# Inverse roots of five norms: one power on GpSimd instead of a root on ScalarE and a reciprocal on VectorE

## The reference

```
h = maximum(layernorm(x), 0)                       # norm 1: (x - m) / sqrt(v + eps)
x = x + L0(h, edges, edge_weight)                  # three gin layers: segment sums and small matmuls
h = maximum(layernorm(x), 0)                       # norm 2
x = x + L1(h, edges, node_vec)
L1: for three layers:                              # widths 256, 256, 128
      res = x @ aw + ab
      x = gat(x, src, dst, gw, a_s, a_d, gb) + res # attention over each node's edges, 8 heads
      x = silu(g * (x - mean) * rsqrt(var + eps) + b)   # batch norm
    x = x @ out_w + out_b
```

## Time and profile before

| | |
|---|---|
| median of 3 runs | 5514.25 us (5514.02 to 5518.28) |
| the profiled execution | 5531.82 us, span 5530.3 us |
| busy: TensorE, VectorE | 2609.5 us (47%), 2382.5 us (43%) |
| busy: ScalarE, GpSimd | 595.1 us (11%), 2781.9 us (50%) |
| table loads on ScalarE at the root's line L688 | 5, of 1283 ns each |

### The profile page before, as it was taken

How to read it: one execution, slowest core, us unless ns; L and a number is a source line. 1 busy time by engine, 2 the same in 40 slices (tenths; PEclk the granted TensorE clock), 3 DMA queues, 4 the chain that set the end, 5 groups by cost and what they waited for, 6 DMA issues and landing times. The chain is left out here.

```text
span 5530.3 us, 62828 instructions
## 1 busy us (share of the span) xinstructions
PE 2609.5 (47%) x13804; PEld 1907.7 (34%) x13804; DVE 2382.5 (43%) x7342; ACT 595.1 (11%) x1968; POOL 2781.9 (50%) x2942
## 2 busy tenths in 40 slices
PE   1666774354545445446355444445543333333333
PEld 1555542123333333334233333333432332332323
DVE  5888513324444444442444444444423333333333
ACT  2222300110000000003000000000020000000001
POOL 2000011356666666663566666666446666666663
PEclk9777887667677766778767677777765555555555
DMA  2222563033333333332333333333312221222222
GB/s 61 106 103 90 242 218 156 26 81 88 89 89 89 89 90 88 91 88 46 81 91 88 89 89 88 88 88 90 67 34 45 47 47 45 47 46 46 46 47 21
DMA packets 246618, 451.19 MB, mean 82 GB/s; under 512 B 163452, under 2 KB 165314, under 8 KB 241709
## 3 DMA queue, kind: packets, MB, share of 16 engines
q0 software_dynamic: 122928, 318.15, 23.6%
q1 hardware_dynamic: 111150, 128.71, 6.9%
q10 hardware_dynamic: 12384, 2.25, 0.3%
HBM read 392.07 MB, written 57.21 MB: 81 GB/s over the span
## 5 line engine op out<-in xcount | busy, mean ns | idle before, releaser
L495 POOL DMA_INDIRECT rows_all<-gat_tab,ell x2664 | 2517.2, 945 | 1566.2 <-issue 799.4
L1003 PE MATMUL banks<-rows_all,ident 128*128 128x264 f32 (+1 forms) x5328 | 1795.9, 506 | 2272.9 <-PEq L119 1791.5
L1003 PEld LDWEIGHTS banks<-rows_all,ident 128*128 128x128 f32 x5328 | 1305.8, 286 | 2763.1 <-issue 2576.9
L1575 DVE COPY lrel<-m_all 128x8 f32 x666 | 133.9, 201 | 1536.2 <-issue 1201.8
L1600 DVE TENSOR_TENSOR rows_all<-rows_all,banks 128x1024 f32<-128x1024 f32 (+1 forms) x666 | 685.7, 1042 | 218.8 <-issue 142.7
L789 ACT ACTIVATE banks<-ex_in 128x40 f32<-128x40 f32 x666 | 138.3, 208 | 3771.3 <-ACTq L119 2499.9
L1553 DVE TENSOR_TENSOR acc<-acc,banks 128x264 f32 (+1 forms) x675 | 259.7, 385 | 469.3 <-DVEq L119 278.1
L1546 DVE TENSOR_TENSOR acc<-acc,banks 128x264 f32 (+1 forms) x675 | 258.0, 382 | 107.0 <-issue 102.3
L859 PE MATMUL banks<-rows_all 128*128 128x52 bf16 x4992 | 187.5, 202 | 157.0 <-PEq L119 151.6
L495 POOL DMA_INDIRECT edges<-sw_d,edge_pick x28 | 34.6, 1236 | 412.5 <-POOLq L119 400.5
L859 PEld LDWEIGHTS banks<-rows_all 128*128 128x128 bf16 x4992 | 176.9, 108 | 182.3 <-issue 181.6
(11 more groups left out here) (276 smaller groups left out, 1974.2 us busy)
## 6 DMA issues: line engine op xcount, KB each, us to landing
rows_all<-gat_tab,ell POOLq DMA_INDIRECT x2664
x_t<-adj_d SPq DMA_DIRECT2D x11, 3328.0 KB
y_t<-adj_d SPq DMA_DIRECT2D x11, 3328.0 KB
adj_d<-x_t SPq DMA_DIRECT2D x7, 3328.0 KB, 10.0
adj_d<-y_t SPq DMA_DIRECT2D x6, 3328.0 KB, 9.8
ell<-ell_d SPq DMA_DIRECT2D x666, 2.5 KB
acc<-key_d SPq DMA_DIRECT2D x1, 1664.0 KB, 6.4
acc<-vec_d SPq DMA_DIRECT2D x1, 1664.0 KB, 18.6
```

Source lines behind the costliest of these rows:

```text
L495: return g.indirect_dma_start(out=dst, out_offset=None, in_=table, in_offset=bass.IndirectOffsetOnAxis(ap=idx, axis=0))
L1003: last = t.matmul(sum_ps[u % SUMS][:, 0:width], ident[:, :], rows[u][:, r * width:(r + 1) * width], start=(r == 0), stop=(r == SLOTS - 1))
```

## The change

GpSimd gets a function `inverse_root`, called five times: behind the 26 gathers of norm 1, behind the 26 gathers of norm 2, and at the end of each attention layer. It waits for the signal (now `root_in`), raises the variance elementwise to a tile of -0.5 and signals `root_done`. VectorE's reciprocals go; the Newton step stays, on the power's result. ScalarE's `sqrt` goes in all five places. In the batch norms a SiLU of one column into an unused tile `warm` stands in its place, so that SiLU's table is loaded there.

```
+        minus_half, warm = sb("minus_half", [P, T]), sb("warm", [P, 1])
...
@@ GpSimd @@
             pool.wait_ge(dst_copied, 16)
 
+            def inverse_root(to, of, n):
+                take(pool, root_in)
+                g.tensor_tensor(to, of, minus_half[:, 0:n], ALU.pow).then_inc(root_done, 1)
+
             take(pool, blk_ready)
             for t in range(T):
                 gather(dst_i[:, t, :], sdst_d.rearrange("(b k) -> b k", k=BLOCK), blk_i[:, t:t + 1]).then_inc(dst_gathered, 16)
 
+            inverse_root(ln_c[:, :], ln_b[:, :], T)
             pool.wait_ge(sw_stored, 32)
...
                 gather(x_res[:, t, :], x1_d, node_i[:, t:t + 1]).then_inc(x_gathered, 16)
+            inverse_root(ln_c[:, :], ln_b[:, :], T)
             for l in range(3):
                 store_rows(gat_tab[l], gat_row[l])
                 rows_all_stored(1 + l)
                 chunk_gathers(l, gat_tab[l], gat_row[l])
+                inverse_root(rstd[:, 0:kout[l]], var[:, 0:kout[l]], kout[l])
...
@@ ScalarE @@
-            def sqrt(n, wide):
-
-                take(act, sqrt_in)
-                s.activation(rtmp[:, 0:wide] if n else ln_c[:, :], var[:, 0:wide] if n else ln_b[:, :],
-                             ACT.Sqrt).then_inc(sqrt_done, 1)
-
-
-            sqrt(0, 0)
-
...
                 last.then_inc(bn_done, 1)
-                sqrt(1, kout[l])
+                s.activation(warm[:, :], half_pi[:, :], ACT.Silu)
                 take(act, silu_in)
...
@@ VectorE @@
+            v.memset(minus_half[:, :], -0.5)
...
                 link(v.tensor_scalar(ln_b[:, :], ln_a[:, :], 1.0 / D, LN_EPS, ALU.mult, ALU.add))
-                signal(sqrt_in)
-                take(dve, sqrt_done)
-                link(v.reciprocal(ln_c[:, :], ln_c[:, :]))
+                signal(root_in)
+                take(dve, root_done)
                 newton(ln_c[:, :], ln_b[:, :], ln_d[:, :])
...
                 link(v.tensor_scalar(var[:, 0:k], bn_sq[:, 0:k], 1.0 / N, BN_EPS, ALU.mult, ALU.add))
-                signal(sqrt_in)
-                take(dve, sqrt_done)
-                link(v.reciprocal(rstd[:, 0:k], rtmp[:, 0:k]))
+                signal(root_in)
+                take(dve, root_done)
                 newton(rstd[:, 0:k], var[:, 0:k], rtmp[:, 0:k])
```

More of the change, by code:

```diff
@@ L357, in program @@
         ht_made, ht_copied, x0_made, x0_added = (sem(n) for n in ("ht_made", "ht_copied", "x0_made", "x0_added"))
-        sqrt_in, sqrt_done, exp_in, exp_done = (sem(n) for n in ("sqrt_in", "sqrt_done", "exp_in", "exp_done"))
+        root_in, root_done, exp_in, exp_done = (sem(n) for n in ("root_in", "root_done", "exp_in", "exp_done"))
         sin_in, sin_done = sem("sin_in"), sem("sin_done")
```

## The result

The changed kernel takes 5539.0 us (median of 8 runs, 5534.8 to 5542.22), the kernel before 5518.34 beside it (8 runs, 5505.1 to 5530.36): 1.0038 times, 95% interval 1.0028 to 1.0047, so 20.7 us or 0.4% slower. Its profiled execution took 5538.18, span 5536.6.

What follows compares the result with a forecast made beforehand. One engine works at a time around the five norms, so changes there count fully. Norm 1 +14.2, `deg_top` all-reduce +5.9, norm 2 +9.8 and batch norms -5.9 give +24.0 on 5514.25: 5538 us, range 5527 to 5549.

Steps and rivals of the forecast that it cites:

- Which engine ends last: At each of the five norms: which engine the others wait for, such as GpSimd's gather queue in norm 1.
- The 0.91 ahead of the weighing: Idle time before the weighing of edges, taken as no cover; as cover, the `deg_top` all-reduce would add 5.0, not 5.9.
- The loads: GpSimd code loads behind the wait: 7.0 us ahead of each 128x26 power, 6.2 ahead of the `deg_top` all-reduce.
- the all-reduce's: At `deg_top`, a code load of 6.2 us delays the all-reduce and adds 5.9 us.
- The power: GpSimd's power takes 4.45 us for 26 columns (0.15 to 9), 0.48 for two, 0.32 for one.
- Norm 1: Load and power come behind the 26 gathers; the cast moves from 98.40 to 112.6, +14.2 us.
- Norm 2: From `ln_b` to Newton 12.0 us instead of 2.19, with load and power uncovered: +9.8.
- Batch norms: Ends of the three layers: root path gives 3.1 us and earlier SiLU 2.8, together -5.9.
- The base: The differences are added to the median of the runs, 5514.25 us, not to the profiled execution's 5531.82.
- A: Rival: GpSimd's code loads don't come again or run ahead of the wait; +4 us, 5518; chance 0.07.
- B: Rival: a cheap power, +13 to +16 us, about 5529; its chance is within the 0.87 for loads on the path.
- C: Rival: shifted code makes one layer's attention loop stop more or less often, 5671 or 5405 us; chance 0.06.

Runs made afterwards that it cites:

- e1: Changed kernel plus three small GpSimd instructions that bring code loads to idle places: 5446.59 us, 1.0012 times the kernel before.
- e8: Changed kernel plus test powers, products and all-reduces on GpSimd behind norm 2's power, all twice: 4869.16 us in one execution.
- e5: The changed kernel again, with no edit: 4784.67 us, 1.0051 times the kernel before.
- e10: The kernel before again, unedited, for a trace: 4755.3 us in one run.
- e6: Kernel before with batch-norm roots on GpSimd, elementwise code and SiLU's table loaded early, and ScalarE's root table early in norm 2: 4757.07 us, 0.9991 times.
- e7: Kernel before plus three unused one-column memsets behind GpSimd's first iotas, to shift its code: 4761.73 us, 1.0001 times.
- e9: The kernel of e1 run again, with no edit: 4769.52 us, 1.0015 times the kernel before.
- e4: Kernel before plus only a one-column SiLU behind ScalarE's root in the batch norms: 5437.42 us, 0.9991 times.

## Why the prediction was right, by its steps

**Which engine ends last** was right in all five norms, and so was what stands behind it. The 0.91 ahead of the weighing was no cover, as chosen.

**The loads** were read rightly from a row without a name. They stand behind the wait (norm 2: 7.74 less the hop of 0.28 is 7.5, where 7.0 stood in the sum), and there are three of them; the all-reduce's added 6.79 - 1.42 = 5.4, where 5.9 stood. e1 shows them by moving them. For the set with the all-reduce e8 has 6.12 and 5.89, and at the kernel's start, less the hop, the twelve traces have 5.9 to 7.8; for the elementwise set the runs show 6.6 to 7.9. These are idle times ahead of the first instruction of the other kind; that a load of code fills them is my reading, no row names it.

**The power**, the softest number, came out near by luck. No run shows the 4.3 us (0.165 a column) that the sum sets on top of the iota's 0.15 for 26 columns, nor the upper bound of 9: both were my guess, and the only slope in a row was the iota's 0.75 ns a column. What the trace shows in their place is 4.53 for 26 columns (4.45 predicted), 0.73 for two (0.48), 0.58 for one (0.32). I had the slope (0.165 against 0.159) and not the base: 0.15 from an iota, where it is 0.3 to 0.4. It made each batch norm 0.25 longer than predicted; shorter hops gave back more than half of that.

**Norm 1** was +14.2 and is +12.6, the largest miss. From the gathers' end to the cast it took 16.49, 0.9 more than the 15.6 predicted (the load again). But the gathers ended 2.5 earlier (94.47 against 96.97), which no step of mine had: 1.8 of it is one gather, told below, and 0.7 is that they began earlier in that execution (59.82 against 60.52). Between e5 and e10 the start lies 0.7 the other way (60.15 against 59.45), and norm 1 is +13.2.

**Norm 2**: +9.8, measured +10.2 (load +0.5, power +0.1, hop back -0.1).

**Batch norms**: -5.9, measured -5.5. SiLU gained 1.29 in two layers as said; the root's path 0.89 instead of 0.99, and 1.03 instead of 1.15. In layer 0 the table load took its 1.28 and no time ahead of it: it starts at 2574.57, where the last square's accumulator read ends (2574.37 + 0.19).

**The base.** Adding to the median and not to the profiled execution was right: spans differ by 6.3, medians by 20.7. From norm 2's Newton to the last `var` the changed kernel took 4384.5 and the one before 4405.8; of these 21 the batch norms explain 4.4. The other 17 lie in the attention loops: the idle time ahead of the neighbour gathers is 1566.2 in one page and 1546.8 in the other. That they are chance of the execution, and no gain of the change, is read from the medians: a lasting gain would leave +6 of the +22.7, and they say +20.7 and, in e5, +23.4. The first execution stood 17.6 over its median on record, 13.5 over that of eight runs.

**Rivals.** A falls (e1, e8). B falls with the power's price. C fell in the form in which I had it: the stops in the attention rounds don't come and go with a few instructions. From norm 2's Newton to the last `mean`, e5, e6, e7, e9 and e10 take 3646.2 to 3651.5, five programs of different code around the loops, and e1 to e4, where those ran, 4298 to 4310. No median moved by near 133. What changes the stops is where the kernel runs, by more than 700 us.

## What to carry to other kernels

A new kind of instruction on GpSimd is priced with the set of code that it needs: count the switches between sets in the order of instructions, 6 to 8 us each here and behind the wait, and put a one-column instruction of that set where the engine is idle. A power there costs 0.16 us a column, good for a few columns on a bare path (0.73 for two) and bad for 26 (4.53). Loading ScalarE's next table behind its last work with a one-column activation is worth the table load, 1.28 here, where the next activation is waited for and ScalarE stands idle 1.5 us before it.

## What the runs showed of the hardware that was not expected

Gathers on GpSimd that run beside a large product of tiles on VectorE took 2.43 and 2.73 us instead of 0.94. Two places in norm 1 of the kernel before; behind the second product comes the clip, which ends at 93.33 + 1.03 = 94.36:

```profile
61.83 1.89 DVE L1165 TENSOR_TENSOR acc<-x_res,ln_a 128x1664 f32<-128x1664 f32 x1
62.11 2.43 POOL L495 DMA_INDIRECT y_t<-sdst_d,blk_i  x1 [0.30 <-issue]
...
91.41 1.89 DVE L1173 TENSOR_TENSOR acc<-acc,ln_c 128x1664 f32<-128x1664 f32 x1
91.75 2.73 POOL L495 DMA_INDIRECT y_t<-sdst_d,blk_i  x1 [0.30 <-issue]
```

The first gather takes 2.43 instead of 0.94 and ends 0.82 behind the two-input instruction (64.54 against 63.72). A gather that begins at 66.77, during a reduction of the same size, takes 0.94. The last one shown takes 2.73 and ends at 94.48, 0.12 behind the clip; in all six traces with ScalarE's root in norm 1 it is 1.85 to 3.03 long and ends 0.11 to 0.12 behind it. In the six traces that have GpSimd's instruction there this product comes after the gathers, and the 26 take 34.6 to 34.7 from first start to last end; in the six with the root 35.6 to 36.7. Why the gather ends 0.12 behind the clip and 0.82 behind a two-input instruction with no clip after it was not found.

The set of code that GpSimd holds, as I read the idle times, seems to outlast an execution. The first iota of the changed kernel:

```profile
1.34 0.15 POOL L507 IOTA id_i<- 128x26 int32 x1 [0.65 <-POOLq L1660]
```

Before it stood at 8.31 behind 7.62 of idle time. The bare instruction stands ahead of it in both. In the four traces of kernels whose last such work is an all-reduce (before, e4, e7, e10) it starts at 8.3 to 8.5, in the eight whose last is a power at 1.34 or 1.35. That fits a set left over from the execution before, and iotas and elementwise work in one set, as the prediction took it. Nothing waits for those 7 us, since the first all-reduce waits for its input until 12.0. No edit was made to test this.

The same kernel took 5518, 5439 and 4761 us in three sets of runs, the last two on chips 2 and 14, with the same gathers. Between the first and the last, 745 of 777 us are idle time ahead of the gathers; that idle time is 820.3 to 821.2 in all six traces of the fastest set, whatever the kernel. What makes TensorE late in the slower sets was not found.
